# A depthwise convolution accumulated in a PSUM slot, the k mean's block products read from PSUM, and new order tables

## The chip, the cores and the metric

One core of a Trainium2 chip runs the kernel. The metric is the device time of one launch in microseconds (us). Shapes are float32 throughout. Engines are TensorE (PE; PEld is its weight load), VectorE (DVE), ScalarE (ACT), GpSimd (POOL) and SyncE (SP), which only issues DMAs.

## What is computed

The input is x, 8 images of 48 channels and 48x48 pixels. Two layers follow each other. The second one (shortened, norms' weights and biases left out) holds all that the change touches:

```python
# layer 0: windowed attention (8x8 windows, 4 heads), gate a * sigmoid(b), 3x3 convolution, residuals
# layer 1:
x = x + dwconv(x, cpe1)
y = ln2d(x); act_res = silu(conv1x1(y, act_proj)); y = conv1x1(y, in_proj)
t = silu(dwconv(y, dwc))                     # tokens, also v
q, k = elu(qk(t)) + 1                        # 6 heads of 8 channels
q_rope, k_rope = rope(q), rope(k)
z = 1 / (q @ mean_over_tokens(k) + 1e-6)     # inside each head
kv = k_rope.T @ v / n
attn = (q_rope @ kv) * z + dwconv(v, lepe)   # lepe: the positional convolution
x = x + conv1x1(attn * act_res, out_proj)
x = x + dwconv(x, cpe2)
x = x + fc2(gelu(fc1(ln2d(x))))
```

## The kernel before

**Tiling.** Two images are worked on together as a pair: image b has channels on partitions 64b to 64b+47, so most tiles have 112 partitions. There are 4 pairs i. Layer 0 goes in 6 strips of 8 rows (`STRIPS`), layer 1 in 3 chunks of 16 rows (`CH`), each 768 pixels. The tiles of layer 1 are `XB` (the residual), `LV` (normalised values, later q·cos), `AR` (the gate), `Q` (in the `QH` tile, shared with fc1's result `HB`), `QS` (q·sin, before that the sums of the `dwc` convolution), `TP` (t with a border), `CT` (two buffers of 768 columns: the positional convolution's sum, then what goes into `out_proj`).

**Jobs and orders.** All work is cut into jobs `name.i.n` (pair i, strip or chunk n). Each engine runs its jobs in the order written out in a table: `PE_ORDER`, `ACT_ORDER`, `DVE_ORDER`, `POOL_ORDER`, `SP_ORDER`. Nothing else reorders; engines meet at semaphores.

**PSUM slots.** PSUM is cut into 4 slots of two banks. A token `f11.2.0@1` in `PE_ORDER` gives TensorE's job the slot 1, and the slots pass from job to job in that order: `wait_slot` waits until the slot's last job was freed by the engine that read it, `filled[k]` and `freed[k]` count. A token `op.3.2@0+20` has TensorE first run 20 filler matmuls (`keep_busy`, line 853: identity times identity into the slot that the job will have, result unused), after the slot's wait and ahead of the job's own waits.

**The part that is changed.** `c20` (ACT, line 1010) writes the middle tap and bias of the positional convolution into `CT`; `c21` to `c28` (DVE, line 1213) add one shifted tap each, 8 per chunk, 96 in all, with `CT` read and written. The `dwc` convolution is done in the same way by `c10` and `c11` to `c18` (lines 1004 and 1203) in `QS`. After `at` (the product with kv, TensorE line 826), `az` (line 1258) multiplies by z into `Q`, and `am` (line 1262) adds `Q` to `CT`; `ym` (POOL, line 1372) multiplies `CT` by the gate and `op` (TensorE, line 596 on `wout_sb`) projects; `oz` (line 1266) adds to `XB`; the DMAs `pz` place it into `XP` for the last depthwise convolution `d3` (TensorE, line 606, 36 matmuls). Behind it come `xc2`, `va2`, `yn2` (norm), three `f1` jobs, `f2` (line 843) and `o` (line 1272).

`kp` (TensorE 792 and 797; DVE 1243 and 1246) makes the two block-diagonal matrices of a pair, `kv_sb` and `km_sb`, by a mask; `dn` (line 813) multiplies q by `km_sb`, and `z` (ACT, lines 1038 and 1040) takes its reciprocal, into `Q`, once `qs` and `qc` have read it. These two are the rope of q on POOL: each is a multiplication by the rows' table and one by the columns' (lines 1338 and 1340), 6 such pairs of instructions for each pair of images. `kr` (lines 1320 and 1327) is the rope of k.

The mask products before:

```python
dve.scalar_tensor_tensor(out=km_sb[:, to], in0=head_blocks[:, 0:C],
                         scalar=slot(job)[0:RG, at:at + 1], in1=head_blocks[:, 0:C],
                         op0=ALU.mult, op1=ALU.mult)
```

## Time and profile before

| | |
|---|---|
| median of 3 runs | 764.94 us (762.53 to 765.15) |
| the profiled execution: its own time | 765.38 us |
| its span, first to last instruction | 763.5 us |
| mean granted TensorE clock | 0.982 |
| busy: PE, PEld | 724.4 us (95%), 460.4 us (60%) |
| busy: DVE, ACT, POOL | 514.0 us (67%), 464.9 us (61%), 297.1 us (39%) |
| HBM read and written | 4.87 MB, 3.54 MB |

Busy time is the time in which an engine has at least one instruction under way. TensorE's counts the fillers too, and its matmuls overlap, so a group's busy time and not its mean times its count says what it takes. An fp32 matmul is two instructions in the profile: the 242 fillers of the table are the x484 of line 853.

### The profile page before, as it was taken

What the parts mean: (1) busy time and instruction counts of PE and PEld (TensorE: products, weight loads), DVE (VectorE), ACT (ScalarE), POOL (GpSimd) and SP (SyncE); (2) the same over time, 40 slices, a digit from 0 to 9 for tenths busy, and PEclk for the clock granted to TensorE, in tenths of its full rate; (3) what the DMA queues carried; (4) which work ended last, traced back from release to release, by engine and by line L of the source; (5) the groups of instructions that cost most, each with busy time, mean ns of one, the idle gap of its engine ahead of it and who ended that gap; (6) DMA issues with size and microseconds to landing.
All of it is one profiled execution on the core that took longest, in us unless ns stands there. A gap on an engine that the chain in (4) does not pass through costs nothing.

```text
span 763.5 us, 19762 instructions
## 1 busy us (share of the span) xinstructions
PE 724.4 (95%) x8464; PEld 460.4 (60%) x8464; DVE 514.0 (67%) x654; ACT 464.9 (61%) x657; POOL 297.1 (39%) x230
## 2 busy tenths in 40 slices
...
PEclk9999999999999999899999999999997989999999
...
GB/s 45 48 74 2 17 17 17 3 1 2 33 17 2 33 17 63 18 17 2 33 26 68 35 17 17 2 2 9 9 22 12 33 17 2 16 33 18 31 17 32
...
## 3 DMA queue, kind: packets, MB, share of 16 engines
...
HBM read 4.87 MB, written 3.54 MB: 11 GB/s over the span
## 4 chain that ended last, share of the span: by engine, by line
PE 73%; DVE 21%; issue 3%; ACT 3%; DVEq 0%; ACTq 0%
PE ps L606 22%; PE ps L596 7%; PE ps L697 7%; DVE CT L1213 7%; PE ps L853 6%; DVE QS L1203 6%; PE ps L672 5%; PE ps L683 3%; PE ps L781 3%; PE ps L843 3%; PE ps L651 2%; PE ps L826 2%; PE ps L660 2%; PE ps L724 2%; PE ps L725 2%
## 5 line engine op out<-in xcount | busy, mean ns | idle before, releaser
L1353 POOL TENSOR_TENSOR SC<-SC,mx 128x768 f32<-128x768 f32 x48 | 75.5, 1575 | 191.0 <-DVE mx L1156 191.0
L606 PE MATMUL ps<-XP,wdw 48*64 48x384 f32 x1728 | 144.4, 483 | 0.9 <-POOL XP L1358 0.6
L1213 DVE SCALAR_TENSOR_TENSOR CT<-TP,vec_sb,CT 112x768 f32<-112x768 f32 x96 | 128.1, 1357 | 1.1
L606 PEld LDWEIGHTS ps<-XP,wdw 48*64 48x64 f32 x1728 | 68.9, 133 | 69.1 <-issue 60.2
L1203 DVE SCALAR_TENSOR_TENSOR QS<-XP,vec_sb,QS 112x768 f32<-112x768 f32 x96 | 100.6, 1092 | 1.1 <-ACT QS L1004 0.7
L1152 DVE TENSOR_TENSOR SC<-ps,bias_sb 128x768 f32<-128x768 f32 x48 | 45.8, 953 | 58.6 <-PE ps L672 58.2
L606 PE MATMUL ps<-G,w_sb 48*64 48x384 f32 x864 | 72.5, 484 | 0.0
L697 PEld LDWEIGHTS ps<-vx,PT 128*128 128x128 f32 x576 | 66.3, 192 | 7.7 <-issue 4.8
L697 PE MATMUL ps<-vx,PT 128*128 128x52 f32 x576 | 68.4, 274 | 0.3 <-ACT PT L938 0.3
L853 PEld LDWEIGHTS ps<-ident_sb 128*128 128x128 f32 x484 | 58.4, 199 | 12.8 <-issue 12.2
L853 PE MATMUL ps<-ident_sb 128*128 128x128 f32 x484 | 63.1, 287 | 0.0
L1051 ACT ACT_TABLE_LOAD x48 | 61.6, 1283 | 0.9
L918 ACT ACTIVATE kx<-ps,hmask_sb 112x384 f32<-112x384 f32 x96 | 47.8, 583 | 18.8 <-DVE qw L1143 18.8
L606 PEld LDWEIGHTS ps<-G,w_sb 48*64 48x64 f32 x864 | 34.5, 132 | 32.6 <-issue 29.0
L934 ACT ACTIVATE SC<-SC 128x768 f32<-128x768 f32 x48 | 40.3, 845 | 22.1 <-POOL SC L1353 21.9
L672 PE MATMUL ps<-kx,qw 48*64 48x256 f32 (+1 forms) x768 | 43.5, 352 | 7.8 <-ACT kx L918 7.4
L1358 POOL TENSOR_TENSOR XP<-XP,YB 112x768 f32<-112x768 f32 x12 | 22.4, 1866 | 72.6 <-DMA YB<-YF 72.6
L1320 POOL TENSOR_TENSOR KX<-KX,rope_th_sb 98x384 f32<-98x384 f32 x12 | 15.7, 1308 | 89.6 <-DVE KX L1220 89.6
L1372 POOL TENSOR_TENSOR CT<-CT,AR 112x768 f32<-112x768 f32 x12 | 23.2, 1938 | 61.1 <-DVE CT L1262 61.1
L1194 DVE TENSOR_TENSOR LV<-LV,XB 112x768 f32<-112x768 f32 x24 | 25.0, 1041 | 32.5 <-ACT LV L987 32.4
L1156 DVE TENSOR_REDUCE mx<-SC 128x12 f32<-128x768 f32 x48 | 45.7, 953 | 1.7
L938 ACT ACTIVATE PT<-ps 128x768 f32<-128x768 f32 x48 | 38.5, 810 | 12.8 <-PE ps L683 12.3
...
## 6 DMA issues: line engine op xcount, KB each, us to landing
...
wln_sb<-in_const_dram SPq DMA_DIRECT2D x6, 9.0 KB
```

Of the source, the lines that this page charges most:

```text
L596: mm = pe.matmul(slot(job)[half(c, HALF), r * BANK:r * BANK + SPX], w[half(r)], src[half(r), c * SPX:(c + 1) * SPX], start=True, stop=True)
L606: mm = pe.matmul(slot(job)[half(c, HALF), r * BANK:r * BANK + SPX], w[half(r), tap * HALF:(tap + 1) * HALF], shifted(t, d * CROWS + c * WI ...
L672: mm = pe.matmul(slot(job)[half(r, HALF), c * BANK + at:c * BANK + at + heads * TOK], qw[n % 2][half(c), w * TOK:(w + 1) * TOK], kx[half(c ...
L697: mm = pe.matmul(o[:, :, hp * 2 * VCOL:(hp + 1) * 2 * VCOL], PT[t // 3][:, k * 128:(k + 1) * 128], va[:, hp, :, w, :], start=True, stop=True)
L853: pe.matmul(slot(job)[:, 0:128], ident_sb[:, :], ident_sb[:, :], start=True, stop=True)
L918: op_ = act.activation(dst[:, h], src, ACT.Identity, scale=head_mask[h])
L1051: act.preload_act_table_set(TABLE[name, i, n])
L1152: dve.tensor_tensor(sc, two(job, 128).rearrange("p b (j m) -> p b j m", m=TOK), bias_sb[:, :].unsqueeze(1).unsqueeze(1).broadcast_to([128, ...
L1156: dve.tensor_reduce(mx[:, (u % NSC) * 12:(u % NSC) * 12 + 12], SC[u % NSC].rearrange("p (j m) -> p j m", m=TOK), AX.X, ALU.max)\
L1203: dve.scalar_tensor_tensor(out=rows16(T0[n]), in0=win, scalar=v(f"dwc_{TAPS[k]}"), in1=rows16(T0[n]), op0=ALU.mult, op1=ALU.add).then_inc( ...
L1213: dve.scalar_tensor_tensor(out=ct, in0=win, scalar=v(f"lepe_{TAPS[k]}"), in1=ct, op0=ALU.mult, op1=ALU.add).then_inc(lepe_step, 1)
L1353: pool.tensor_tensor(sc, sc, bc_last(mx[:, (u % NSC) * 12:(u % NSC) * 12 + 12], TOK), ALU.subtract).then_inc(sub_ready, 1)
```

## The change

The positional convolution is summed in a PSUM slot. A new TensorE job `h2.i.n`, 12 in all, does no matmul: it waits for its slot and increments `filled`. `c20` waits for that in place of the wait that frees `CT`, and writes the slot; `c21` to `c28` read and write the slot; `am` adds `Q` to the slot into `CT` and frees it, and has the wait for `CT` now (the `op` of two chunks ago). The semaphore `am_ready` is gone, and who waited for it (`ym`, and the gelu jobs) waits for the slot's release. `kp` now makes `kv_sb` by one `scalar_tensor_tensor` over both images and `km_sb` by one `tensor_tensor` whose first operand is the column in PSUM, broadcast. All five order tables are new: the PE table holds 503 jobs for 491, and 113 fillers for 242; the ACT table makes the kernel load 54 activation tables where it loaded 48.

```diff
@@ -377,7 +379,6 @@
         qhalf_ready = sem("qhalf_ready")
         qs_ready = sem("qs_ready")
         qc_ready = sem("qc_ready")
-        am_ready = sem("am_ready")
         ym_ready = sem("ym_ready")
 
         def slot(job):
@@ -414,6 +415,9 @@
 
         def chunk(t, d):
             return t[0:RG, d * CPX:(d + 1) * CPX]
+
+        def eights(ap):
+            return ap.rearrange("p (b y) x -> p b y x", b=2)
 
         def pairs(ap):
             return ap.rearrange("p (b n) -> p b n", b=2)
@@ -747,6 +751,9 @@
                 elif name in ("ip", "ac"):
                     pe.wait_ge(yn_ready, i * CH + n + 1)
                     turned(job, w_inp if name == "ip" else w_act, chunk(LV[i % 2], n))
+                elif name in ("h1", "h2"):
+                    wait_slot(pe, job)
+                    pe.sem_inc(fill(job), 1)
                 elif name == "kt":
                     pe.wait_ge(t_ready, i * CH + n + 1)
                     wait_slot(pe, job)
@@ -1005,9 +1012,8 @@
                                    scale=v(f"dwc_{TAPS[0]}"), bias=v("dwc_b")).then_inc(dwc_begun, 1)
                 elif name == "c20":
                     act.wait_ge(t_ready, i * CH + halo_last(n) + 1)
-                    if kc >= 2:
-                        wait_filled(act, ("op", (kc - 2) // CH, (kc - 2) % CH))
-                    act.activation(rows16(CT[kc % 2]), shifted(TP, n * CROWS, CROWS, TAPS[0])[0:RG], ACT.Identity,
+                    wait_filled(act, ("h2", i, n))
+                    act.activation(two8(("h2", i, n)), eights(shifted(TP, n * CROWS, CROWS, TAPS[0])[0:RG]), ACT.Identity,
                                    scale=v(f"lepe_{TAPS[0]}"), bias=v("lepe_b")).then_inc(lepe_begun, 1)
                 elif name == "ts":
                     act.wait_ge(dwc_step, DWC_STEP[8, i, n])
@@ -1042,7 +1048,8 @@
                     m = int(name[2])
                     job = (f"f1{m}", i, n)
                     wait_filled(act, job)
-                    act.wait_ge(am_ready, (i + 1) * CH)
+                    for d in range(CH):
+                        wait_read(act, ("h2", i, d))
                     act.activation(pairs(HB[:, m, :]), two(job, 128), ACT.Gelu, bias=fc1b2[:, m:m + 1])\
                        .then_inc(free(job), 2)
 
@@ -1205,12 +1212,12 @@
                 elif name[:2] == "c2":
                     k = int(name[2])
                     win = shifted(TP, n * CROWS, CROWS, TAPS[k])[0:RG]
-                    ct = rows16(CT[kc % 2])
+                    t = two8(("h2", i, n))
                     if k == 1:
                         dve.wait_ge(lepe_begun, LEPE_BEGUN[i, n])
                     else:
                         dve.wait_ge(lepe_step, LEPE_STEP[k - 1, i, n])
-                    dve.scalar_tensor_tensor(out=ct, in0=win, scalar=v(f"lepe_{TAPS[k]}"), in1=ct,
+                    dve.scalar_tensor_tensor(out=t, in0=eights(win), scalar=v(f"lepe_{TAPS[k]}"), in1=t,
                                              op0=ALU.mult, op1=ALU.add).then_inc(lepe_step, 1)
                 elif name == "ko":
                     job = ("kt", i, n)
@@ -1237,16 +1244,12 @@
                 elif name == "kp":
                     job = ("kp", i, n)
                     wait_filled(dve, job)
-                    for b in range(2):
-                        to = slice(b * HALF, b * HALF + C)
-                        at = b * BANK + HALF
-                        dve.scalar_tensor_tensor(out=km_sb[:, to], in0=head_blocks[:, 0:C],
-                                                 scalar=slot(job)[0:RG, at:at + 1], in1=head_blocks[:, 0:C],
-                                                 op0=ALU.mult, op1=ALU.mult)
-                        op_ = dve.scalar_tensor_tensor(out=kv_sb[:, to], in0=slot(job)[0:RG, b * BANK:b * BANK + C],
-                                                       scalar=1.0 / PX, in1=head_blocks[:, 0:C],
-                                                       op0=ALU.mult, op1=ALU.mult)
-                    op_.then_inc(free(job), 2)
+                    blocks = bc_mid(head_blocks[:, 0:C], 2)
+                    images = lambda t: t[:, :].rearrange("p (b c) -> p b c", b=2)[:, :, 0:C]
+                    kv, km = two(job, n=C), two(job, n=HALF + 1)[:, :, HALF:HALF + 1].broadcast_to([RG, 2, C])
+                    dve.scalar_tensor_tensor(out=images(kv_sb), in0=kv, scalar=1.0 / PX, in1=blocks,
+                                             op0=ALU.mult, op1=ALU.mult)
+                    dve.tensor_tensor(images(km_sb), km, blocks, ALU.mult).then_inc(free(job), 2)
                 elif name == "kk":
                     job = ("kk", i, n)
                     wait_filled(dve, job)
@@ -1259,7 +1262,10 @@
                 elif name == "am":
                     wait_read(dve, ("at", i, n))
                     dve.wait_ge(lepe_step, LEPE_STEP[8, i, n])
-                    dve.tensor_tensor(CT[kc % 2], CT[kc % 2], chunk(Q, n), ALU.add).then_inc(am_ready, 1)
+                    if kc >= 2:
+                        wait_filled(dve, ("op", (kc - 2) // CH, (kc - 2) % CH))
+                    job = ("h2", i, n)
+                    dve.tensor_tensor(pairs(CT[kc % 2]), two(job), pairs(chunk(Q, n)), ALU.add).then_inc(free(job), 2)
                 elif name == "oz":
                     job = ("op", i, n)
                     wait_filled(dve, job)
@@ -1367,7 +1373,7 @@
                     wait_filled(pool, ("ac", i, n))
                     q_rope(i, n, 0, qc_ready)
                 elif name == "ym":
-                    pool.wait_ge(am_ready, kc + 1)
+                    wait_read(pool, ("h2", i, n))
                     wait_read(pool, ("ac", i, n))
                     pool.tensor_tensor(CT[kc % 2], CT[kc % 2], chunk(AR, n), ALU.mult).then_inc(ym_ready, 1)
```

Of the order tables, the end of `PE_ORDER` alone:

```diff
-    kt.3.2@0 f12.2.2@3 f11.2.2@2 f10.2.2@0 f2.2.2@3+6 kv.3.1@2 q.3.0@0 q.3.1@1 q.3.2@3 kv.3.2@2+9 kp.3.0@0+2
-    kk.3.0@1+5 dn.3.0@3 dn.3.1@2 dn.3.2@0 at.3.0@1+29 at.3.1@3+7 at.3.2@1+9 op.3.0@2+2 op.3.1@3+4 d3.3.0@0+31
...
+    f10.2.2@2 f12.2.2@1 kv.3.1@2 vt.3.2@0 f2.2.2@1 q.3.0@2 q.3.1@0 q.3.2@1 kv.3.2@2 h2.3.1@0 h2.3.2@1 kp.3.0@2
+    kk.3.0@2 dn.3.0@2 at.3.0@2 dn.3.1@2 at.3.1@3 at.3.2@2 op.3.0@3 dn.3.2@0 op.3.1@3 op.3.2@0+20 d3.3.0@3+3
```

TensorE in the last pair, from `dn` (L813, now L820) on; L853, now L860, are the fillers, L826 (L833) is `at`, and `wout_sb` stands in `op`. Before:

```order
L813 MATMUL ps<-QH,km_sb 64x384 x12
L853 MATMUL ps<-ident_sb 128x128 x29
L826 MATMUL ps<-LV,kv_sb 64x384 x4
L826 MATMUL ps<-QS,kv_sb 64x384 x4
L853 MATMUL ps<-ident_sb 128x128 x7
L826 MATMUL ps<-LV,kv_sb 64x384 x4
L826 MATMUL ps<-QS,kv_sb 64x384 x4
L853 MATMUL ps<-ident_sb 128x128 x9
L826 MATMUL ps<-LV,kv_sb 64x384 x4
L826 MATMUL ps<-QS,kv_sb 64x384 x4
L853 MATMUL ps<-ident_sb 128x128 x2
L596 MATMUL ps<-CT,wout_sb 64x384 x4
```

and now:

```order
L820 MATMUL ps<-QH,km_sb 64x384 x4
L833 MATMUL ps<-LV,kv_sb 64x384 x4
L833 MATMUL ps<-QS,kv_sb 64x384 x4
L820 MATMUL ps<-QH,km_sb 64x384 x4
L833 MATMUL ps<-LV,kv_sb 64x384 x4
L833 MATMUL ps<-QS,kv_sb 64x384 x4
L833 MATMUL ps<-LV,kv_sb 64x384 x4
L833 MATMUL ps<-QS,kv_sb 64x384 x4
L600 MATMUL ps<-CT,wout_sb 64x384 x4
L820 MATMUL ps<-QH,km_sb 64x384 x4
L600 MATMUL ps<-CT,wout_sb 64x384 x4
L860 MATMUL ps<-ident_sb 128x128 x20
```

`dn` is split: its first job goes ahead of `at.3.0`, its last behind `at.3.2` and the first `op`, since it takes the slot that `h2.3.1` had. The 29, 7, 9, 2 and 4 fillers are gone, and 20 stand ahead of the last `op`.

VectorE in the last pair. L1258 (now L1261) is `az`, L1262 (L1268) `am`, L1266 (L1272) `oz`, L1213 (L1220) a tap. Before:

```order
L1262 TENSOR_TENSOR CT<-CT,QH 112x768
L1258 TENSOR_TENSOR QH<-ps,QH 112x768
L1266 SCALAR_TENSOR_TENSOR XB<-ps,vec_sb,XB 112x768
L1213 SCALAR_TENSOR_TENSOR CT<-TP,vec_sb,CT 112x768
L1266 SCALAR_TENSOR_TENSOR XB<-ps,vec_sb,XB 112x768
L1213 SCALAR_TENSOR_TENSOR CT<-TP,vec_sb,CT 112x768 x7
L1262 TENSOR_TENSOR CT<-CT,QH 112x768
L1266 SCALAR_TENSOR_TENSOR XB<-ps,vec_sb,XB 112x768
```

and now:

```order
L1220 SCALAR_TENSOR_TENSOR ps<-TP,vec_sb,ps 112x2x384
L1256 COPY kv_sb<-ps 112x128
L1220 SCALAR_TENSOR_TENSOR ps<-TP,vec_sb,ps 112x2x384 x7
L1261 TENSOR_TENSOR QH<-ps,QH 112x768
L1220 SCALAR_TENSOR_TENSOR ps<-TP,vec_sb,ps 112x2x384 x4
L1268 TENSOR_TENSOR CT<-ps,QH 112x768
L1220 SCALAR_TENSOR_TENSOR ps<-TP,vec_sb,ps 112x2x384 x3
L1261 TENSOR_TENSOR QH<-ps,QH 112x768
L1268 TENSOR_TENSOR CT<-ps,QH 112x768
L1272 SCALAR_TENSOR_TENSOR XB<-ps,vec_sb,XB 112x768 x2
L1261 TENSOR_TENSOR QH<-ps,QH 112x768
L1268 TENSOR_TENSOR CT<-ps,QH 112x768
```

The 8 taps of the last chunk stood behind the second chunk's `am` and the first `oz`; now they stand ahead of the first `am` and the second `az`, mixed with the taps of the second chunk.

GpSimd in the last pair, rope of q: L1338 and L1340 (now L1344 and L1346), `LV` in `qc` and `QS` in `qs`. Before:

```order
L1338 TENSOR_TENSOR LV<-QH,rope_y_sb 112x768
L1340 TENSOR_TENSOR LV<-LV,rope_x_sb 112x768
L1338 TENSOR_TENSOR LV<-QH,rope_y_sb 112x768
L1340 TENSOR_TENSOR LV<-LV,rope_x_sb 112x768
L1338 TENSOR_TENSOR QS<-QH,rope_y_sb 112x768
L1340 TENSOR_TENSOR QS<-QS,rope_x_sb 112x768
```

and now:

```order
L1344 TENSOR_TENSOR LV<-QH,rope_y_sb 112x768
L1346 TENSOR_TENSOR LV<-LV,rope_x_sb 112x768
L1344 TENSOR_TENSOR QS<-QH,rope_y_sb 112x768
L1346 TENSOR_TENSOR QS<-QS,rope_x_sb 112x768
L1344 TENSOR_TENSOR QS<-QH,rope_y_sb 112x768
L1346 TENSOR_TENSOR QS<-QS,rope_x_sb 112x768
L1344 TENSOR_TENSOR QS<-QH,rope_y_sb 112x768
L1346 TENSOR_TENSOR QS<-QS,rope_x_sb 112x768
L1344 TENSOR_TENSOR LV<-QH,rope_y_sb 112x768
L1346 TENSOR_TENSOR LV<-LV,rope_x_sb 112x768
```

Before, the three `qc` go first and then the three `qs`; now chunk 0 has both its halves first, and the last to come is a `qc`. The count is the same.

## Rows read from the trace of the kernel before

**Rows 1.** Page, parts 1, 2 and 4: busy time, granted clock, last chain.

```profile
PE 724.4 (95%) x8464; PEld 460.4 (60%) x8464; DVE 514.0 (67%) x654; ACT 464.9 (61%) x657; POOL 297.1 (39%) x230
...
PEclk9999999999999999899999999999997989999999
...
PE 73%; DVE 21%; issue 3%; ACT 3%; DVEq 0%; ACTq 0%
```

**Rows 2.** Busy time by stretch; last come clock, DMA share, GB/s.

```profile
250.00:310.00 60.00, 55.47 (x603) 31.73 (x598) 59.27 (x61) 47.94 (x56) 9.88 (x6) 0.97 0.18 36
555.00:585.00 30.00, 26.48 (x314) 12.53 (x310) 27.01 (x20) 10.34 (x11) 29.61 (x17) 0.90 0.08 21
672.00:695.00 23.00, 22.01 (x236) 17.12 (x238) 9.49 (x14) 5.98 (x7) 22.52 (x15) 1.00 0.05 14
695.00:764.00 69.00, 63.95 (x666) 40.60 (x658) 22.17 (x22) 24.45 (x27) 5.45 (x3) 0.99 0.12 27
```

**Rows 3.** The same view for line 853 alone: the filler matmuls.

```profile
250.00:280.00 30.00, 10.85 (x90) 10.27 (x90) 1.00 0.17 31
620.00:672.00 52.00, 6.97 (x46) 6.59 (x46) 0.94 0.08 19
672.00:695.00 23.00, 12.94 (x104) 11.99 (x104) 1.00 0.05 14
695.00:764.00 69.00, 25.92 (x206) 23.82 (x206) 0.99 0.12 27
```

**Rows 4.** Groups by line: taps, fillers, table loads, mask products, `qo`.

```profile
L1213 DVE SCALAR_TENSOR_TENSOR CT<-TP,vec_sb,CT 112x768 f32<-112x768 f32 x96 | 128.1, 1357 | 1.1
...
L853 PE MATMUL ps<-ident_sb 128*128 128x128 f32 x484 | 63.1, 287 | 0.0
L1051 ACT ACT_TABLE_LOAD x48 | 61.6, 1283 | 0.9
...
L1243 DVE SCALAR_TENSOR_TENSOR km_sb<-wln_sb,ps 112x48 f32<-112x48 f32 x8 | 10.6, 1328 | 2.5 <-PE ps L797 2.5
...
L1226 DVE SCALAR_TENSOR_TENSOR QH<-QH,ps 112x768 f32<-112x768 f32 x12 | 11.2, 945 | 0.6 <-ACT QH L1027 0.5
...
L1246 DVE SCALAR_TENSOR_TENSOR kv_sb<-ps,wln_sb 112x48 f32<-112x48 f32 x8 | 1.6, 195 | 0.0
```

**Rows 5.** Views of L1213 and L1266: shortest, median, longest in ns.

```profile
L1213 DVE SCALAR_TENSOR_TENSOR CT<-TP,vec_sb,CT x96: 1004/1019/2577, 203.6 to 710.3; 112x768 f32<-112x768 f32 x96
...
L1266 DVE SCALAR_TENSOR_TENSOR XB<-ps,vec_sb,XB x12: 1001/1010/1018, 253.1 to 717.0; 112x768 f32<-112x768 f32 x12
```

**Rows 6.** Timeline at 562 to 580 us: start, duration, GpSimd, then VectorE.

```profile
563.60 2.20 POOL L1338 TENSOR_TENSOR QS<-QH,rope_y_sb 112x768 f32<-112x768 f32 x1
565.87 2.42 POOL L1340 TENSOR_TENSOR QS<-QS,rope_x_sb 112x768 f32<-112x768 f32 x1
...
564.60 11.49 DVE L1213 SCALAR_TENSOR_TENSOR CT<-TP,vec_sb,CT 112x768 f32<-112x768 f32 x5
```

**Rows 7.** Timeline, last pair, GpSimd: rope of q, first and last.

```profile
674.99 1.48 POOL L1338 TENSOR_TENSOR LV<-QH,rope_y_sb 112x768 f32<-112x768 f32 x1
...
693.18 1.82 POOL L1340 TENSOR_TENSOR QS<-QS,rope_x_sb 112x768 f32<-112x768 f32 x1
```

**Rows 8.** Timeline of the end, 672 us on.

```profile
672.04 2.17 PE L764 MATMUL ps<-TP,wlq_sb 49*64 49x384 f32 x24
...
703.99 7.33 DVE L1213 SCALAR_TENSOR_TENSOR CT<-TP,vec_sb,CT 112x768 f32<-112x768 f32 x7
...
712.46 1.82 POOL L1372 TENSOR_TENSOR CT<-CT,AR 112x768 f32<-112x768 f32 x1 [12.05 <-DVE CT L1262]
...
759.31 1.02 DVE L1272 SCALAR_TENSOR_TENSOR XB<-ps,vec_sb,XB 112x768 f32<-112x768 f32 x1 [4.55 <-PE ps L843]
```

**Rows 9.** Who waited for whom: TensorE.

```profile
PEld ps L813 <- DVE kv_sb L1246: 4.7, 2, 3.5
...
PE ps L596 <- DVE KX L1220: 2.6, 2, 1.5
```

More of the change, by code:

```diff
@@ L102 @@
[L102 to L106 removed]
+    qk.0.0@0 v.0.0@1 sc0.0.0@2 sc1.0.0@3 s1.0.0@0 qk.0.1@1 v.0.1@2 tr0.0.0@0+8 sc0.0.1@2+4 sc1.0.1@3 qk.0.2@1
@@ new lines @@
+    pt0.1.4 ie.0.1 ie.0.2 pt1.1.4 c10.0.0 ex0.1.5 c10.0.1 c10.0.2 oe.1.3 ex1.1.5 sg.1.1 pt0.1.5 ed.1.1 oe.1.4
+    ar.0.0 sg.1.2 sg.1.3 ed.1.2 sg.1.4 ed.1.3 ed.1.4 yf.1.0 ts.0.0 yf.1.1 ke.0.0 ve.0.0 pt1.1.5 qe.0.0 ts.0.1
+    ar.0.1 ar.0.2 qe.0.1 ke.0.1 ve.0.1 ts.0.2 c20.0.0 oe.1.5 ke.0.2 qe.0.2 x3.1.0 ve.0.2 c20.0.1 sg.1.5 ed.1.5
+    z.0.0 yf.1.2 z.0.1 z.0.2 c20.0.2 x3.1.1 x3.1.2 sq.1.0 x4.0.0 rs.1.0 sq.1.1 sq.1.2 sq2.0.0 rs.1.1 rs.1.2
+    ie.1.0 ar.1.0 x4.0.1 ar.1.1 ar.1.2 sq2.0.1 xw.2.0 xw.2.1 x4.0.2 kx.2.0 vx.2.0 vx.2.1 sq2.0.2 xw.2.2 xw.2.3
@@ new lines @@
+    ge2.1.2 kx.3.4 ex1.3.3 oe.3.2 pt0.3.3 sg.3.1 vx.3.4 ed.3.1 ex0.3.4 sg.3.2 ed.3.2 pt1.3.3 sq.2.0 ex1.3.4
+    kx.3.5 yf.3.0 rs.2.0 pt0.3.4 ex0.3.5 vx.3.5 pt1.3.4 sq.2.1 oe.3.3 sq.2.2 rs.2.1 rs.2.2 ex1.3.5 sg.3.3 ar.2.0
+    pt0.3.5 ar.2.1 ed.3.3 ar.2.2 oe.3.4 pt1.3.5 ie.2.0 ie.2.1 c10.2.0 sg.3.4 ie.2.2 oe.3.5 c10.2.1 c10.2.2
+    ed.3.4 sg.3.5 ed.3.5 yf.3.1 ts.2.0 yf.3.2 ke.2.0 qe.2.0 ts.2.1 x3.3.0 qe.2.1 ke.2.1 ve.2.0 ve.2.1 c20.2.0
+    ts.2.2 x3.3.1 ke.2.2 x3.3.2 qe.2.2 ve.2.2 c20.2.1 sq.3.0 rs.3.0 z.2.0 z.2.1 z.2.2 c20.2.2 sq.3.1 ie.3.0
```

225 lines of the change are left out of this document (107 added, 118 removed).

## The prediction

> **What bounds the kernel now.** I read the page first. TensorE is busy 95% of the span and carries 73% of the chain that ended last, VectorE 21% [rows 1]. But TensorE's 724.4 us hold 63.1 us of fillers, 242 of them at 0.261 us [rows 4]. With 763.5 − 724.4 = 39.1 us idle that makes 102 us in which TensorE waits for others. Everything to be won lies there, so the second view is where these 102 us stand: fillers of 10.9 us at 250 to 280 us, 7.0 at 620 to 672, and 12.9 + 25.9 from 672 us on, where the last pair's q step begins and no other pair is left to fill in [rows 3, 8]. The third view is what the other engines do there. From 250 to 310 us VectorE is busy 59.3 of 60 us; from 555 to 585 us GpSimd is busy 29.6 of 30; from 672 to 695 us GpSimd again, 22.5 of 23 [rows 2]. So the waits belong to VectorE and GpSimd, stage by stage.
>
> The fourth view is why these two are slow. A tap of the positional convolution has a median of 1.02 us but a mean of 1.36 [rows 4, 5]. Five of them take 11.5 us at 564 us, 2.3 us each, and beside them GpSimd's rope steps take 2.20 and 2.42 us [rows 6], where they take 1.48 and 1.82 with VectorE quiet [rows 7]. Each waits for the other in turn. L1226 and L1266, each with one input in PSUM, never leave 0.94 to 1.02 us, whatever GpSimd does [rows 4, 5]; so a sum in PSUM should free the taps. The Trainium skill, page "SBUF — State Buffer", section "Who interferes with whom", says that a VectorE instruction with two SBUF inputs and a GpSimd instruction that reads SBUF exclude each other, and one with at most one SBUF input does not contend. By that rule the taps are freed; the trace agrees.
>
> **The change part by part.**
>
> *The taps.* 96 instructions, count unchanged. None in the trace reads and writes PSUM in one instruction, so the price is bounded: 0.945 us as L1226, and 1.357 us, the mean that a tap has now [rows 4], if the relief fails. I take 1.02, as the quiet tap and L1266 have it [rows 5]. That frees 96 × 0.34 = 32 us of VectorE, and the 12 `am` in the same way some 4 us. The Trainium skill speaks against the change here: its page "VectorE: DVE Perf Modes", section on the TRN2 errata, gives a PSUM source 62 cycles of fixed cost more than an SBUF source; by an estimate from that page 96 taps would cost 6.2 us more. The quiet tap's 1.02 beside L1266's 1.01 shows no such difference [rows 5], so the sum goes without it.
>
> *The mask products.* Now four instructions per pair, (10.6 + 1.6) / 4 = 3.05 us, since each L1243 multiplies two SBUF operands and is caught by GpSimd [rows 4]. After: two with one operand in PSUM, of 96 elements. Bounds 0.2 (L1246, 48 elements) and 0.9 us (L1226, 768 elements) each; I take 0.25. So `dn` can come 2.5 us sooner in each pair. TensorE waited for it twice, 4.7 us together [rows 9]. I count **−4 us**; the last pair's is hidden by the rope.
>
> *The new order at the end.* From 672.0 us (the q step) to the last rope's end at 693.18 + 1.82 = 695.0, GpSimd is the bound [rows 7, 8]. The change has the same six ropes there (12 instructions, 19.8 us) and the same work ahead of them, so these 23 us stay. But in that stage VectorE is busy only 9.5 of 23 us [rows 2], and the 8 taps of the last chunk come after it, 7.3 us at 704 to 711, so that the last `ym` starts at 712.5, 17 us after the ropes' end [rows 8]. In the change all taps stand ahead of the second `az`. They are 18 behind the q step, 18 × 1.02 = 18.4 us, which fits under the ropes only because the two no longer contend. What is late next is the last chunk's chain: the last `dn` needs the slot that the second `am` frees, then `z`, `az`, `am`, `ym`, `op`.
>
> From the ropes' end TensorE has 63.95 − 25.9 = 38.0 us of needed work, 25.9 us of fillers, and 68.5 − 63.95 = 4.6 us idle, nearly all of it the last `o` and store, 763.5 − 759.3 = 4.2 us [rows 2, 3, 8]. After the change the needed work is the same within a `dn` (0.7 us), the end is the same 4.6, and 55 fillers are left in that part (20 ahead of the last `op`, then 3, 8, 6, 12, 6): 14.4 us. The 20 with the jobs between cover that chain. 38.0 + 14.4 + 4.6 = 57.0 for 68.5: **−11.5 us**.
>
> *Fillers before that.* 87 before, 58 now: 29 × 0.261 = **−7.6 us**, where the waits under them are shorter. Most were at 250 to 280 us, VectorE's full stage, and at 620 to 672 [rows 2, 3]; the freed VectorE and GpSimd time falls in the stages ahead of these. That the fillers went is no proof that the waits did; the 36 us freed on VectorE are more than the 7.6 I take.
>
> *The slots.* 12 `h2` jobs, each holding one of 4 slots for 6 to 20 of TensorE's jobs, 155 in sum (counted in the table). TensorE waits at an `h2` for the slot, and everything behind it in its queue waits too; `c20` on ScalarE waits for the grant, and `ke`, `qe` and `ve` stand behind it. The trace has few waits for a slot: two of 1.3 us behind L1220 [rows 9]. Bounds: 0, and one such wait for every hold, 12 × 1.3 = 16 us. The orders put the holds where TensorE's large jobs stand (`d0`, `d3`, `cv`), so I take 0 and keep 16.
>
> *Small things.* 6 more table loads are 6 × 1.28 = 7.7 us of ScalarE [rows 4], which is busy 61% and 10.3 of 30 us in the rope stage [rows 1, 2]: 0, and 7.7 if that cover is gone. The k mean's wait moved to `am` (for `op` of two chunks ago) stands where that `op` is long done: 0. `c20` into PSUM: 0. The 29, 7 and 9 fillers ahead of the three `at` are gone and the clock may fall: from 555 to 585 us it is 0.90 on the mean [rows 2], which of the two levels, 1.2 and 2.4 GHz, is 6 us at the lower, costing 3. I take 0, and 3 for the range.
>
> **Sum.** −11.5 − 7.6 − 4 = −23.1. The profiled execution's own time is 765.4 (0.4 above the median of the runs), so 742.3; against the median 741.8. I say 742.
>
> **The rivals.**
>
> *More is freed.* All 129 fillers go with their waits, 129 × 0.261 = 33.7 us, 731.7, and with them a quarter of TensorE's idle time ahead of 672 us, 39.1 − 1.0 − 4.6 = 33.5 us [rows 2]: 723 to 724. For it: VectorE and GpSimd shorten in every rope stage, on which I counted little. Against: the 160 us of VectorE in the chain, 21% [rows 1], are mostly the `dwc` taps and the quiet stretch from 250 to 310 us, where a tap costs 1.02 already.
>
> *Nothing is gained.* TensorE needs its 724.4 − 63.1 = 661 us and the idle places only move: the 11.5 us at the end come, and short slots give them back. 764.
>
> *Slower, by the slots.* With one slot held for 155 of 503 jobs, three carry the rest. Each wait of TensorE on a slot costs 1.3 us [rows 9]; the gain is used up at 23.1 / 1.3 = 18 of them, and at 30 (two or three in each hold) the kernel is at 742.3 + 39 = 781. It would show as TensorE's matmuls waiting on DVE and ACT readers of `ps`. The Trainium skill's page "PSUM — Partial Sum Buffer", summary of rules, tells authors to evacuate promptly because PSUM is tight, which is this rival. Against: TensorE hardly waits for slots now.
>
> *The relief fails.* A PSUM sum costs 1.36 a tap: 18 taps are 24.4 us and end 4.6 us behind the ropes, and the DVE-bound stages keep their waits: −23.1 + 4.6 + 7.6 = −11, 754.
>
> **How the numbers follow.** Forecast 0.58, more freed 0.14, relief fails 0.06: all faster. Nothing gained 0.10. Slower 0.12. A measurement of this kernel can tell about 0.5%, 3.8 us. So faster 0.78, same 0.10, slower 0.12. The range: below it goes to the second case, 724. Above, the forecast with one wait for each hold and the clock's 3 is 742 + 19 = 761; the no-gain case takes it to 764.
>
> **What would show it.** Right: taps of 1.0 us with no spread; rope steps of 1.5 and 1.8 us beside them; mask products under 0.3 us; ropes' end to the span's end near 57 us; line 860 (the fillers) near 29.5 us. Wrong: TensorE's idle time above 60 us, its waits naming readers of `ps`; taps above 1.2 us; the last `ym` more than 10 us after the ropes' end; a clock of 0.5 over the last pair's `at` and `d3`.

## The result and the profile after it

The changed kernel takes 801.55 us (median of 5 runs, 800.78 to 805.19) against 765.15 us (5 runs, 762.53 to 771.39): a ratio of 1.05, 95% interval 1.0468 to 1.0531, so it is slower by 5%. Forecast were 742 us and a range of 724 to 764. The profiled execution has a span of 803.4 us. Of the runs below, one execution of old_free (3204 us) and one of orders_sbuf4 (851 us) were in a slower state and are left out of the medians.

The page of the changed kernel, parts 1, 2 and 4, answers to [rows 1]:

```profile
PE 735.5 (92%) x8206; PEld 451.2 (56%) x8206; DVE 471.4 (59%) x646; ACT 471.8 (59%) x663; POOL 276.2 (34%) x230
...
PEclk9979999699999997967799899999998999996799
...
PE 31%; ACT 4%; DVE 4%; issue 3%; POOL 1%; DMA 0%; SPq 0%; ACTq 0%; DVEq 0%
```

VectorE has lost 42.6 us of work and GpSimd 20.9, as the relief promised, and the kernel is 40 us longer all the same. The granted clock is the first thing to see: it has dips where it had hardly any.

The relief itself is complete. The line and tile views of the changed kernel answer to [rows 4] and [rows 5]; the three numbers behind "x96:" are the shortest, median and longest in ns:

```profile
L1220 DVE SCALAR_TENSOR_TENSOR ps<-TP,vec_sb,ps x96: 1008/1017/1024, 218.0 to 740.6; 112x768 f32<-112x768 f32 x96
```

```profile
L1268 DVE TENSOR_TENSOR CT<-ps,QH 112x768 f32<-112x768 f32 x12 | 11.5, 955 | 1.3 <-DVE ps L1220 0.8
...
L860 PE MATMUL ps<-ident_sb 128*128 128x128 f32 x226 | 33.6, 305 | 0.7 <-ACT QH L1053 0.6
...
L1250 DVE SCALAR_TENSOR_TENSOR kv_sb<-ps,wln_sb 112x96 f32<-112x96 f32 x4 | 1.0, 248 | 0.0
L1252 DVE TENSOR_TENSOR km_sb<-ps,wln_sb 112x96 f32<-112x96 f32 x4 | 1.0, 247 | 0.0
```

A tap never takes more than 1.024 us; `am` takes 0.955 on the mean, a mask product 0.25. The ropes of q have medians of 1.48 and 1.81 us over the whole program, and only one step of the first kind took more, 2.185 us at 642.3 us (shown are the `qs` halves; the longest `qc` steps took 1.50 and 1.83):

```profile
L1344 POOL TENSOR_TENSOR QS<-QH,rope_y_sb x12: 1467/1476/2185, 215.9 to 731.7; 112x768 f32<-112x768 f32 x12
L1346 POOL TENSOR_TENSOR QS<-QS,rope_x_sb x12: 1805/1814/1828, 217.4 to 733.2; 112x768 f32<-112x768 f32 x12
```

**Where the time went.** Three prices make up what TensorE does not need: its fillers, its idle time (span minus busy) and the lower clock, span × (1 − granted clock). Before they are 63.1, 39.1 and 763.5 × 0.018 = 13.7 us, after 33.6, 67.9 and 803.4 × 0.072 = 57.8. The rest, 647.6 and 644.1 us, is the same work. The third price is an upper bound, since it counts the lower clock over idle time too; where there is much of both, the rest comes out too small (629.1 us in orders_sbuf below). So fillers and idle time together, which I call the waits, went from 102.2 to 101.5, and by this account the clock took up to 44 us, a little more than the 39.9 by which the span grew.

To see where, I lined the two traces up by TensorE's progress (its busy time without the fillers, each stretch at the lower clock counted half); such figures are good to some 2 us. The change is behind by 5 us at 50 us of the kernel before, by 12 at 150, 15 at 300, 34 at 400, 42 at 450, 45 at 650 and 40 at 740. Busy time by stretch, first of the kernel before, then of the change over the same work (370 to 492 us); the columns are those of [rows 2]:

```profile
350.00:400.00 50.00, 48.75 (x570) 28.85 (x566) 37.06 (x51) 34.55 (x54) 21.55 (x13) 1.00 0.11 20
400.00:450.00 50.00, 49.87 (x606) 29.34 (x598) 22.51 (x34) 36.06 (x50) 10.52 (x7) 1.00 0.19 43
```

```profile
370.00:434.00 64.00, 58.23 (x611) 31.93 (x611) 46.10 (x61) 30.74 (x48) 19.50 (x13) 0.84 0.12 23
434.00:492.00 58.00, 53.37 (x618) 32.42 (x614) 22.57 (x36) 40.60 (x61) 11.12 (x7) 0.94 0.12 28
...
718.60:741.70 23.10, 13.85 (x138) 5.78 (x130) 21.26 (x26) 8.15 (x10) 21.13 (x16) 0.70 0.05 13
741.70:803.40 61.70, 56.61 (x566) 31.80 (x566) 12.62 (x13) 22.85 (x26) 5.35 (x3) 0.91 0.14 30
```

From 370 to 492 us TensorE is idle 10.4 us, where it was idle 1.4, and loses 64 × 0.16 + 58 × 0.06 = 13.7 us to the clock, where it lost nothing. In neither kernel is there a filler in this stretch. The last two rows are the stage on which I had counted most: it comes 47 us late, and is itself 6.8 us shorter than before.

### The profile page after: what moved, and what is told of

Same layout as the page of the kernel before. It is cut to its first block and busy times, and to the rows that moved or that the text cites. A ratio compares the mean times of both kernels' runs of the same rounds, so it can differ in the third digit from the quotient of the medians.

```text
span 803.4 us, 19304 instructions
## 1 busy us (share of the span) xinstructions
PE 735.5 (92%) x8206; PEld 451.2 (56%) x8206; DVE 471.4 (59%) x646; ACT 471.8 (59%) x663; POOL 276.2 (34%) x230
## 5 line engine op out<-in xcount | busy, mean ns | idle before, releaser
L1359 POOL TENSOR_TENSOR SC<-SC,mx 128x768 f32<-128x768 f32 x48 | 73.7, 1536 | 277.5 <-DVE mx L1163 277.5
L610 PE MATMUL ps<-XP,wdw 48*64 48x384 f32 x1728 | 146.8, 491 | 5.4 <-POOL XP L1364 4.0
L1159 DVE TENSOR_TENSOR SC<-ps,bias_sb 128x768 f32<-128x768 f32 x48 | 45.8, 954 | 92.6 <-PE ps L676 92.4
L1220 DVE SCALAR_TENSOR_TENSOR ps<-TP,vec_sb,ps 112x768 f32<-112x768 f32 x96 | 95.9, 1017 | 5.1 <-ACT ps L1016 3.4
L1364 POOL TENSOR_TENSOR XP<-XP,YB 112x768 f32<-112x768 f32 x12 | 29.7, 2478 | 87.6 <-DMA YB<-YF 87.6
L945 ACT ACTIVATE PT<-ps 128x768 f32<-128x768 f32 x48 | 38.7, 810 | 30.7 <-PE ps L687 30.4
L687 PE MATMUL ps<-ident_sb,SC 128*128 128x128 f32 x288 | 45.8, 303 | 4.7 <-ACT LV L992 2.0
L1201 DVE TENSOR_TENSOR LV<-LV,XB 112x768 f32<-112x768 f32 x24 | 28.0, 1171 | 36.5 <-ACT LV L994 36.4
L687 PEld LDWEIGHTS ps<-ident_sb,SC 128*128 128x128 f32 x288 | 36.5, 158 | 17.6 <-issue 16.7
L978 ACT ACTIVATE XB<-ps,vec_sb 112x768 f32<-112x768 f32 x12 | 10.8, 901 | 55.8 <-PE ps L610 32.8
```

The lines of the kernel that those rows point to most:

```text
L610: mm = pe.matmul(slot(job)[half(c, HALF), r * BANK:r * BANK + SPX], w[half(r), tap * HALF:(tap + 1) * HALF], shifted(t, d * CROWS + c * WI ...
L687: mm = pe.transpose(slot(job)[:, j * 128:(j + 1) * 128], SC[u % NSC][:, j * 128:(j + 1) * 128], ident_sb[:, :])
L1159: dve.tensor_tensor(sc, two(job, 128).rearrange("p b (j m) -> p b j m", m=TOK), bias_sb[:, :].unsqueeze(1).unsqueeze(1).broadcast_to([128, ...
L1220: dve.scalar_tensor_tensor(out=t, in0=eights(win), scalar=v(f"lepe_{TAPS[k]}"), in1=t, op0=ALU.mult, op1=ALU.add).then_inc(lepe_step, 1)
L1359: pool.tensor_tensor(sc, sc, bc_last(mx[:, (u % NSC) * 12:(u % NSC) * 12 + 12], TOK), ALU.subtract).then_inc(sub_ready, 1)
```

## The experiments

Seventeen kernels ran. The table has each run's median, its ratio to the kernel before on the same chip with the 95% interval, and the account as above (fillers, idle time, clock loss, in us of the profiled execution).

| run | us | ratio | interval | fillers | idle | clock |
|---|---|---|---|---|---|---|
| before | 765.15 | 1 | | 63.1 | 39.1 | 13.7 |
| the change | 801.55 | 1.05 | 1.0468–1.0531 | 33.6 | 67.9 | 57.8 |
| before_kp | 761.87 | 0.9961 | 0.9936–0.9987 | 63.5 | 38.7 | 9.9 |
| orders_sbuf | 850.75 | 1.1151 | 1.1118–1.1184 | 34.4 | 105.5 | 78.8 |
| hold_sbuf | 850.60 | 1.117 | 1.1103–1.1237 | 32.6 | 98.4 | 87.5 |
| orders_sbuf4 | 838.48 | 1.101 | 1.0944–1.1075 | 33.8 | 108.5 | 66.9 |
| after_reslot | 802.64 | 1.05 | 1.0462–1.0539 | 32.2 | 69.5 | 57.0 |
| before_nofill | 778.07 | 1.0193 | 1.0165–1.0222 | 0 | 80.7 | 50.5 |
| after_nofill | 810.97 | 1.0633 | 1.0576–1.0691 | 0 | 92.6 | 68.0 |
| kp_fill | 761.51 | 0.9963 | 0.9931–0.9996 | 69.7 | 30.5 | 15.3 |
| orders_free | 790.69 | 1.0331 | 1.0238–1.0424 | 31.0 | 72.0 | 34.4 |
| orders_free_hold | 794.16 | 1.0373 | 1.0296–1.0449 | 34.3 | 68.1 | 47.7 |
| old_free | 750.39 | 0.9814 | 0.9741–0.9887 | 61.6 | 32.2 | 6.7 |
| hyb3 | 752.91 | 0.9857 | 0.9823–0.9892 | 36.5 | 46.8 | 21.0 |
| hyb3_sbuf | 768.96 | 1.0064 | 1.0038–1.0091 | 37.5 | 60.4 | 26.0 |
| hyb23 | 770.99 | 1.0086 | 1.0054–1.0119 | 42.3 | 53.2 | 27.7 |
| new0b | 802.36 | 1.046 | 1.0405–1.0514 | 61.9 | 60.4 | 41.0 |
| hyb3_12 | 754.22 | 0.989 | 0.9856–0.9923 | 37.6 | 48.3 | 19.5 |
| hyb3_2 | 762.24 | 0.9966 | 0.9943–0.9989 | 35.2 | 56.5 | 26.6 |

### One part at a time

**before_kp**: the kernel before with the new mask products alone.

```diff
-                    for b in range(2):
...
+                    dve.scalar_tensor_tensor(out=images(kv_sb), in0=kv, scalar=1.0 / PX, in1=blocks, ...)
+                    dve.tensor_tensor(images(km_sb), km, blocks, ALU.mult).then_inc(free(job), 2)
```

> The kernel before with the new mask products alone (two instructions with one operand in PSUM for four). Forecast: mask products 0.25 us each, TensorE's wait for them 4.7 us less, 761 us. Rival: the waits are taken up elsewhere, within 0.5% of before.

It gains 2.6 us by the medians on the same chip (764.45 to 761.87), where I had put down 4. That is within the rival's 0.5% as well, and the waits speak for the rival in part: TensorE's 4.6 us of waits for `kv_sb` are gone, but in the two profiled executions its idle time went only from 39.1 to 38.7 us.

**orders_sbuf**: the change's five order tables and mask products, and no `h2`: the sum stays in SBUF, in three buffers instead of two, since in these orders the sum of the third chunk begins before the first is read. To make room, the second set of scaled identities is left out and the first used twice, so one set-up instruction is missing and the second residual's depthwise weights are others; so it is in every run below that stands on this one. **hold_sbuf**: the same, but the `h2` jobs are there and hold their slots empty.

```diff
-                    act.activation(two8(("h2", i, n)), eights(...), ...)
+                    act.activation(rows16(CT[n]), shifted(...)[0:RG], ...)
```

> The changed kernel's five orders and mask products, but the convolution's sum back in SBUF: no h2 jobs, no held slots. A third CT buffer takes the place of the slot's freedom; to make room for it the last depthwise convolution runs with the weights of the first (same matmuls, other values) and one VectorE instruction of the setup is left out. Theory S (held slots make TensorE wait, and the short waits pull the clock down): the waits go with the slots, time under the lower clock falls from 119 us to below 60, time 765 to 775 us although the taps contend with GpSimd again (mean tap above 1.2 us). Rival O (the new orders with their 113 fillers are themselves at fault): 795 to 805 us, lower clock still above 90 us.

> As orders_sbuf, but the h2 jobs are back: each slot is granted before the convolution's first tap and freed by am, and nothing reads or writes it between; the sum stands in SBUF. Same weights left out. Theory S: as slow as the change or slower, 800 to 815 us, since the slots are held and the taps contend as well. Rival O: equal to orders_sbuf within 1%. If a PSUM sum itself cost something, this one would be faster than the change.

Both take 851 us, more than either theory gave for orders_sbuf. Source view of the tap of orders_sbuf:

```profile
L1208 DVE SCALAR_TENSOR_TENSOR CT<-TP,vec_sb,CT x96: 1005/1210/5428, 216.8 to 786.1; 112x768 f32<-112x768 f32 x96
```

Under the new orders the taps stand beside GpSimd far more: their mean is 1.50 us, one took 5.4. So within these orders the sum in PSUM is worth 49 us (850.75 − 801.55), and a slot that is held costs nothing beside one that is not. One flaw: orders_sbuf kept the change's dealing of jobs to slots, so the slot that `h2` would have held stood empty, and the two could hardly differ. **orders_sbuf4** deals the jobs anew over all four slots; **after_reslot** deals the change's own anew, by the times of its trace.

```diff
-    ... h2.1.0@3 h2.1.1@0 kk.1.0@1 dn.1.0@2 dn.1.1@1 ...
+    the same jobs in the same order, other numbers behind @
```

> orders_sbuf with its slots dealt out anew over all four (each job takes the slot that has been free longest by the trace of orders_sbuf), in place of the change's dealing, in which a slot stood empty where h2 had held it; same weights left out. Theory S (three slots for the rest is what costs): 830 us or less, from 851, idle TensorE time down by 15 us or more. Rival O (the new orders wait for data, not for slots): 845 to 855 us.

> The changed kernel with its slots dealt out anew, each job and each h2 the slot that has been free longest by the trace of the change; order and fillers the same. If the dealing was at fault, 790 us or less. Theory S (slots are short whoever has which): 797 to 805 us.

orders_sbuf4 came between the two theories: its ratio is 1.101 for the 1.1151 of orders_sbuf, so the fourth slot gives back about 11 us of the 86, though TensorE's idle time does not fall (105.5 to 108.5 us). A new dealing of the change gives nothing. So a slot less is a small part of the loss in these two kernels, and the dealing is none.

### The fillers

**before_nofill** and **after_nofill** leave out every filler (the "+" numbers of the PE table):

```diff
-    ... at.3.0@1+29 at.3.1@3+7 at.3.2@1+9 ...
+    ... at.3.0@1 at.3.1@3 at.3.2@1 ...
```

> The kernel before with its 242 filler matmuls removed and nothing else. Theory C (fillers hold the clock up in the waits): time under the lower clock rises from 30 us to above 80 us and the kernel takes 780 to 800 us. Rival (fillers only use up waits, as my forecast priced them): 758 to 766 us, with the clock where it was.

> The changed kernel with its 113 fillers removed. before_nofill showed 14 us for 242 fillers. Theory C (fillers hold up the clock where they stand): 805 to 815 us. Rival: they only lengthen waits that have grown short, 795 to 801 us. Set beside before_nofill (778 us) it gives the change without any fillers: if it is 20 us or more slower than that, missing fillers are not the whole of the loss.

Cores view of before_nofill, span and granted clock:

```profile
core 0: 777.5 us, clock 0.935
```

63.1 us of fillers are gone, 41.6 of idle time and 36.8 of clock loss have come: by the medians fillers are worth about 14 us before and 9 after. Without any filler the change is still 33 us behind the kernel before, so its fewer fillers explain about 4 of the 36 us and no more. **kp_fill** adds 24 fillers to before_kp, some into a slot other than the next job's; at 761.5 us it fits neither theory's number and shows nothing that before_kp does not.

```diff
+                if (name, i, n) in FILL:
+                    fill_free((name, i, n))
```

> before_kp (761.9 us) with 24 more fillers in the waits of TensorE over 0.4 us that its trace has and where a slot is free. Theory C: each wait filled saves a spell of the lower clock, 757 to 760 us, clock 0.995. Rival: 762 us or more, the fillers delaying the jobs behind them.

### Orders against slots, with contention taken out

**orders_free**, **orders_free_hold** and **old_free** put a reduction with one SBUF operand in place of each tap and of the addition of Q. The sum of the positional convolution and that addition are left out; count and place of the instructions stay, and nothing is left for GpSimd to exclude.

```diff
-                    dve.scalar_tensor_tensor(out=ct, in0=win, scalar=v(f"lepe_{TAPS[k]}"), in1=ct,
-                                             op0=ALU.mult, op1=ALU.add).then_inc(lepe_step, 1)
+                    dve.tensor_reduce(ct[:, :, 0], win, AX.X, ALU.max).then_inc(lepe_step, 1)
```

> The new orders and the new mask products, no held slot, jobs dealt over all four slots; each tap is one VectorE reduction over the same window with one SBUF operand, and so is the addition of Q (left out: the positional convolution's sum and the addition of Q; same number of VectorE instructions, about 0.95 us each, nothing for GpSimd to contend with). It is the changed kernel with the relief and without the hold. If the shortage of slots made the changed kernel slow, it comes to 765 us or less, for the 40.8 us of TensorE's waits at four full slots shrink towards the 15 of before. If the new orders are at fault by themselves, it stays at 790 to 805.

> As the kernel before it in this list, with the slots held and the jobs dealt as in the change (left out: the same sum and addition of Q). Both theories expect the changed kernel's time, 795 to 805 us, since its taps cost about the same; if it comes out well below, the sum's time in PSUM itself, or its reads of PSUM beside TensorE's writes, is part of the loss. Its distance from the kernel before is the price of the hold with quiet taps: 0 if the orders are at fault, 30 or more if the slots are.

> The old orders with the new mask products, and with the same one-operand reductions for taps and addition of Q (left out: that sum and that addition). What the relief alone gives without any new order: 96 taps and 12 additions at about 0.95 us instead of 1.36 and 1.3. If the waits belong to VectorE and GpSimd as the prediction said, 725 to 745 us; if the old orders were fitted so closely to their own durations that shorter steps bring nothing, 755 to 762.

Page lines and cores view of old_free, then of orders_free with one stretch of it (the same work as 370 to 434 us of the change):

```profile
L1213 DVE TENSOR_REDUCE CT<-TP 112x16 f32<-112x768 f32 x96 | 88.9, 948 | 2.6 <-ACT CT L1010 1.3
...
core 0: 748.5 us, clock 0.991
```

```profile
L1208 DVE TENSOR_REDUCE CT<-TP 112x16 f32<-112x768 f32 x96 | 89.5, 950 | 4.5 <-ACT CT L1005 2.8
...
core 0: 782.4 us, clock 0.956
...
361.00:424.00 63.00, 55.18 (x588) 29.99 (x592) 42.71 (x58) 28.70 (x44) 19.50 (x13) 0.86 0.12 24
```

This is the experiment that settles it. With equal taps, equal mask products and no slot held, the new orders take 790.7 us and the old ones 750.4, by the ratios 5.2% apart. Beside the order they differ in what belongs to the new tables, 129 fillers fewer (about 4 us by the two kernels without fillers) and six table loads (7.7 us of ScalarE), and in the third buffer with its missing set-up instruction. The hold adds 3.5 us by the medians; the intervals overlap and would allow up to 12. Even with it orders_free_hold is 7 to 10 us below the change, whose taps take 1.017 us where the reductions take 0.95. The stretch that is slow in the change is slow here too: 7.8 us idle and a clock of 0.86, and 6.0 of the 7.8 are `op` waiting for `ym`. So the new tables are at fault, whatever the instructions cost; no run parts the five tables from each other. old_free also says what the relief is worth where the orders are not touched: about 11 us beyond before_kp, not the 23 of the forecast, and between the two numbers expected (725 to 745, 755 to 762). At equal progress it is 1 us behind the kernel before at 300 us, past VectorE's full stretch, where the taps are quiet anyway, level with it at 550, and 9 and 12 us ahead at 600 and 650: the relief pays between 550 and 650 us, where the third pair's ropes of q stand. At 700 it is still 12: in the last pair's ropes of q, which the kernel before runs at 1.48 and 1.82 us already, nothing is added.

### Where the orders lose, and the end alone

The next kernels join two sets of orders: every engine does what one set has up to a time in its trace, then what is left in the other set's sequence. PSUM sums stand only in the part with the new orders, the mask products are new everywhere.

```diff
+                    t = two8(("h2", i, n)) if (i, n) in INPS else eights(rows16(CT[kc % 2]))
```

**hyb3**: old orders to 647 us, the change's for the last pair, its three sums in PSUM. **hyb3_sbuf**: the same with the sum in SBUF.

> The old orders with the new mask products up to 647 us, where the last pair's positional convolution begins; from there the change's orders with the sum in a held slot, for the last pair alone; pairs 0 to 2 keep the sum in SBUF. If the change's loss lies in its orders for the middle of the program, only the gain at the end is left, 6.8 of the 11.5 us that were forecast there: 761.9 - 6.8 = 755, and 750 to 757 us in all. If holding slots or the end's new order cost time in themselves, which the change's other gains hid, it stays at 762 or above.

> As the kernel before it in this list, but the last pair's sum stays in SBUF too, in three buffers (the second set of scaled identities is left out and the first used twice, which leaves one set-up instruction out and changes the depthwise weights of the second residual). It parts the order of the end from the relief. If the end gains because the taps no longer exclude GpSimd's ropes, it loses the gain and comes to 762 to 770 us: 18 taps of 1.9 and the ropes of 2.2 and 2.4 us beside each other. If the order alone brings it, 757 us or less.

Timeline of hyb3 (GpSimd: a q rope in the last pair, and the last one's end), then the same two ropes in hyb3_sbuf:

```profile
673.36 1.48 POOL L1358 TENSOR_TENSOR QS<-QH,rope_y_sb 112x768 f32<-112x768 f32 x1
674.91 1.81 POOL L1360 TENSOR_TENSOR QS<-QS,rope_x_sb 112x768 f32<-112x768 f32 x1
...
688.20 1.81 POOL L1360 TENSOR_TENSOR LV<-LV,rope_x_sb 112x768 f32<-112x768 f32 x1
```

```profile
673.10 2.19 POOL L1357 TENSOR_TENSOR QS<-QH,rope_y_sb 112x768 f32<-112x768 f32 x1
675.36 2.40 POOL L1359 TENSOR_TENSOR QS<-QS,rope_x_sb 112x768 f32<-112x768 f32 x1
...
693.85 2.40 POOL L1359 TENSOR_TENSOR LV<-LV,rope_x_sb 112x768 f32<-112x768 f32 x1
```

Both theories' numbers for hyb3 were apart, and it hit the first: 752.9 us, 1.4% faster than the kernel before (interval 0.9823 to 0.9892) and faster than before_kp. With the sum in SBUF the same order is slower than before, 769.0. So the new end pays, and only with the relief: in SBUF its taps raise five of the six ropes of q to 2.19 and 2.40 us, in PSUM none.

**hyb23**: old orders to 537 us, then the change's, PSUM sums in pairs 2 and 3. **new0b**: the change's to 290 us, PSUM sums in pair 0, then the old ones.

> The old orders with the new mask products up to 537 us, from there the change's orders with the sum in a held slot for pairs 2 and 3. At equal progress of TensorE the change lies 42 us behind the kernel before at 450 us of the latter and still 42 us at 600: if the loss is made in the orders ahead of 450 us, this kernel has none of it, 755 to 763 us. If the new orders lose everywhere in proportion, the last 30% of them cost 12 us: 775 us or more.

> The other way round: the change's orders, with the sum in a held slot for pair 0, up to 290 us, and the old orders with the new mask products behind them, sums in SBUF. By the lag at equal progress, 15 us at 300 us of the kernel before, it comes to 762 + 15 = 777, 772 to 782 us, if orders cost what they cost where they stand, whatever follows. If the loss up to there was only work put off, and is made good by the old orders behind, 762 to 767 us.

Both missed. hyb23 is 18 us slower than hyb3; at equal progress 10 of these come between 500 and 550 us, right behind the join. new0b has the change's lag up to its join (16 us at 250) and 32 more between 250 and 350, again at the join. A join leaves jobs that one order does early and the other late, and these two can't part its price from that of the orders. They agree with the lag that the new orders lose time ahead of 290 us; that the stretch from 350 to 450 us costs 21 us rests on the lag and the rows above, and on its coming back in orders_free, not on them.

**hyb3_12** and **hyb3_2** give back one and two of hyb3's three held slots, with those chunks summed in SBUF.

```diff
-        INPS = [(3, 0), (3, 1), (3, 2)]
+        INPS = [(3, 1), (3, 2)]
```

> As hyb3, but of the last pair's three chunks only the second and third sum in PSUM; the first stays in SBUF, and its slot is free for TensorE's jobs from 652 to 686 us. In hyb3 all three sums hold a slot at once, one slot is left from 672 to 687 us, and TensorE waits there 1.7 us for the first at, 1.6 for the second dn and 2.9 for the second at while that slot is read. If the held slots cost this, it gains up to 6 us: 747 to 750 us. If those waits are for the mask products, z and the ropes, which one more slot doesn't hasten, and the first chunk's eight taps in SBUF exclude GpSimd's k ropes again, it loses 2 to 6 us: 755 to 759.

> As hyb3, but only the third chunk sums in PSUM; the first two stay in SBUF. Held slots: 747 us or less, as one hold is left. Relief: between hyb3 (752.9) and the SBUF version (769.0), nearer to the latter as 8 more of the 18 taps stand beside the q ropes: 760 to 766.

Timeline of hyb3, TensorE, where one slot is left; in brackets the wait ahead of the job and who ended it:

```profile
677.94 1.56 PE L836 MATMUL ps<-LV,kv_sb 48*64 48x384 f32 x8 [1.87 <-ACT QH L1051]
...
682.54 1.56 PE L823 MATMUL ps<-QH,km_sb 48*64 48x384 f32 x8 [1.76 <-DVE QH L1271]
...
687.10 1.56 PE L836 MATMUL ps<-LV,kv_sb 48*64 48x384 f32 x8 [3.00 <-DVE CT L1279]
```

These look like the slot waits of my rival, 6.6 us together. With one slot more hyb3_12 takes 754.2 us, between its two forecasts, and its interval and hyb3's overlap. Its timeline in the same place:

```profile
687.49 1.56 PE L836 MATMUL ps<-LV,kv_sb 48*64 48x384 f32 x8 [5.86 <-POOL LV L1360]
```

The three waits are one now, for GpSimd's rope, and TensorE is busy 13.6 of 23 us in this stage for 13.8. So the slot was what each wait ended with, and the rope what TensorE waited for; the slots broke that wait into pieces. In hyb3 the rope of the second `at` ended at 684.88 + 1.80 = 686.68 us, 0.4 us before that `at` began, so the slot itself cost 0.4 there. In hyb3_12 the last rope ends 1.3 us later than in hyb3, since the k ropes stand beside the first chunk's taps in SBUF, and what the fourth slot gives may hide behind that. hyb3_2 came to 762.2, inside what the relief theory gave (760 to 766).

Not tried: the PSUM sum for all pairs in the old orders. There the time from `c20` to `am` is 11 to 71 us a chunk, and in every pair two slots would be held at once for 41 to 66 us. Not tried either: the last pair's PSUM sums under the old order of the end, which would say what hyb3 owes to its order beside the relief.

## Why the prediction failed, point by point

**The taps and mask products** were right in size: 1.017 us for the 1.02 taken, 0.25 for 0.25, ropes 1.48 and 1.81. The Trainium skill, page "SBUF — State Buffer", section "Who interferes with whom", agrees from both sides: no tap in the change is held up, and of 48 rope steps of q the one that is, 2.185 us, stands beside a VectorE instruction with two SBUF operands (L1201, `LV<-LV,XB`, 1.87 us); in hyb3_sbuf the ropes are at 2.19 and 2.40 us again. The other page's fixed cost for a PSUM source ("VectorE: DVE Perf Modes", section on the TRN2 errata) does not show: 1.017 against the quiet SBUF tap's 1.019. **−4** for the mask products is 2.6 in before_kp, and TensorE's idle time hardly fell with it.

**"From the ropes' end"**, forecast 57.0 for 68.5. The ropes' end is at 739.86 + 1.81 = 741.7 us, 23 us after the q step as forecast, and from there it is 61.7 us: −6.8 for −11.5. The timeline of the change, last rope and last `ym`:

```profile
739.86 1.81 POOL L1346 TENSOR_TENSOR LV<-LV,rope_x_sb 112x768 f32<-112x768 f32 x1
...
751.87 1.81 POOL L1378 TENSOR_TENSOR CT<-CT,AR 112x768 f32<-112x768 f32 x1 [6.22 <-DVE CT L1268]
```

The last chunk's chain, which I had named as late next, starts its `ym` 10.2 us after the ropes' end, just past the 10 that I had put down as a sign of being wrong. The 4.7 us missed are about what the clock took: 0.91 over this stretch, 5.6 us, for the 0.7 of before. In hyb3 the same end takes 60.0 us.

**"The clock: I take 0, and 3 for the range"** is the term that was mis-sized most. I priced it at one place. The fillers of [rows 3] had kept TensorE busy 22.01 of 23 us in the rope stage, at 1.00 [rows 2]; without them it is busy 13.85 of 23.1, and the granted clock is 0.70 there. But the larger part fell elsewhere, much of it where no filler had stood: 370 to 434 us at 0.84. Over the run it is up to 44 us.

**"Fillers before that: −7.6."** The 58 fillers are there as counted (18.3 us ahead of the q step, 15.3 behind the ropes' end). I had written that their going was no proof that the waits did, and took the gain all the same. The waits did not go: 29.5 us less of fillers, 28.8 more of idle time. And at this idle time stands the lower clock. That fillers in the same places would have held it is my conclusion from before_nofill; no run put fillers into the change's waits. **The failed step is this one**: I priced the tables' new sequence by the fillers that they ask for. I looked at the old trace's waits at the end, and for the other 600 us assumed that the sequence keeps TensorE fed as well as before. orders_free, 40 us over old_free, is the price of that assumption.

**"The slots: I take 0"** held roughly, within the 16 us that I kept for it: 3.5 us with quiet taps (up to 12 by the intervals), some 11 for the fourth slot in SBUF, dealing anew 0, one given back at the end nothing that shows. The slower rival at 781 had the right side and the wrong mechanism. Its sign came (TensorE idle 67.9 us, above 60, as `PE ps L833 <- DVE CT L1268: 4.1, 3, 3.0` of the waits view), but a wait that ends with a slot's reader does not say that the slot was what lacked: orders_free has the idle time without any hold. So the PSUM page's summary ("PSUM — Partial Sum Buffer" in the Trainium skill: evacuate promptly) is not what decided here.

**The relief's worth.** I had tied the gains at the end and ahead of it to relief and order together, 19.1 us. The relief alone gives about 11 in the old orders, and the new order of the last pair with the relief there 9.0 (before_kp to hyb3). "More is freed" was farther off still. The rival "the relief fails" fell with the first row of the taps.

What stays open is how the 40 us divide over the five tables. One place can be read from the traces, though no run changed it alone. In the second pair the old VectorE table has no tap between `kp.1.0` and `am.1.0`; the new one has 10 ahead of `az.1.0` (the first of them at 372.27 us, then the nine shown) and 4 behind it. VectorE in the kernel before, `az` right behind its `at`; then in the change, with TensorE's stretch around it; then `op` in orders_free, where the same 14 reductions stand:

```profile
357.60 0.96 DVE L1258 TENSOR_TENSOR QH<-ps,QH 112x768 f32<-112x768 f32 x1 [0.83 <-PE ps L826]
358.59 1.23 DVE L1262 TENSOR_TENSOR CT<-CT,QH 112x768 f32<-112x768 f32 x1
```

```profile
373.40 8.41 DVE L1220 SCALAR_TENSOR_TENSOR ps<-TP,vec_sb,ps 112x768 f32<-112x768 f32 x9
381.72 0.95 DVE L1261 TENSOR_TENSOR QH<-ps,QH 112x768 f32<-112x768 f32 x1
382.59 3.79 DVE L1220 SCALAR_TENSOR_TENSOR ps<-TP,vec_sb,ps 112x768 f32<-112x768 f32 x4
386.28 0.95 DVE L1268 TENSOR_TENSOR CT<-ps,QH 112x768 f32<-112x768 f32 x1
...
373.00:393.00 20.00, 17.63 (x118) 7.42 (x118) 19.76 (x24) 9.93 (x12) 8.65 (x6) 0.50 0.00 1
```

```profile
376.93 1.56 PE L591 MATMUL ps<-CT,wout_sb 48*64 48x384 f32 x8 [5.21 <-POOL CT L1362]
```

VectorE is busy 46 of 64 us from 370 to 434, but 19.76 of the 20 in which `am` and `op` are due, and there the granted clock is 0.50: half of these 20 us is nearly all that the clock takes in the 64. The waits themselves are short in the change (1.7 us for `am`, 1.5 for a mask product, 1.5 for `XP`), since TensorE, at the lower clock, comes late to them; orders_free, whose groups of eight matmuls for `at` take 0.82 us there and the change's 1.53, shows the wait at its full length. The same mixing of taps gains time in the last pair, where GpSimd's ropes are what TensorE waits for.
